# SiLU on ScalarE, six pooled products and alternating score banks in a scan, attention and experts kernel

## The chip, the cores and the metric

The program runs on one core of one Trainium2 chip. The metric is the device time of one launch in microseconds (us), all three stages included. The units of work are TensorE (PE), VectorE (DVE), ScalarE (ACT), GpSimd (POOL) and the DMA queue of SyncE (SP).

## The reference, cut to what matters

The input is 4 images of 64 channels and 1024 positions. Three stages follow each other.

```
for each of 8 sequences (4 images, plain and with the channels shuffled):
    u   = silu(conv(x @ W_in.T) + conv_b)               # 1024 x 128
    B, C, dt_low = u @ W_x.T;  dt = softplus(dt_low @ W_dt.T + b_dt)
    for n in 16 states: h_n[t] = exp(dt*A_n)[t] * h_n[t-1] + (dt*u*B_n)[t]
    y   = (sum over n of h_n * C_n + u * D_skip) * silu(z) @ W_out.T
t = t + causal_attention(layernorm(t))                   # 4 x 1024 x 64
t = t + experts(layernorm(t))                            # attention and feed-forward steps, picked by an argmax
```

## The kernel before

**The scan stage** (`build_scan`) takes the 8 sequences one after the other, and in each the 16 states ("units"). A unit is one 128 x 1024 tile: the channels on the partitions, the positions along the free axis. ScalarE makes the decay exp(dt*A_n) (line 474). The drive dt*u*B_n is made in one of two ways. For the 7 units in `POOLED` GpSimd multiplies a copy of B_n that a DMA has spread over the partitions (line 764); it goes to `dbu`, and the decay then goes to one of the two PSUM tiles `pb`. For the 9 others TensorE spreads B_n into `pb` (line 246), VectorE multiplies it by dtu there (line 618), and the decay goes to one of three `da` tiles. VectorE scans (line 623), GpSimd multiplies by C_n (`hc`, line 753), and TensorE adds the 16 results up in `py` (line 257).

**The next sequence is prepared meanwhile** in two PSUM banks `px`, one for each half of 512 positions, which every step reuses in a fixed order: the convolution (198, 199), Tanh and Identity on ScalarE (409, 410), u on VectorE (582), B and C and their bf16 parts (205 to 218), dt (224 to 230, with 432 to 451 on ScalarE and 589 on VectorE), dt*u (599), then z of the current sequence (236), Tanh (455) and the gate (605). After units 0 to 2 of the next sequence VectorE reads `py` (631). Once in two sequences, at units 13 to 15, TensorE also makes the output of an image (266, 271).

Every engine runs one queue in the order of the code. Each loop over u makes, on its engine, first what the unit needs and then the steps whose `n ==` matches; semaphores hold an engine until its operands are there. TensorE's turn at unit u is: the spread of B for unit u+1 (which waits until scan u-1 is done), the sum of unit u-3, then the steps. ScalarE's is: the decay of u+1, then the steps.

**Attention** (`Attention`, 16 groups of 128 queries, once causal as `l_`, then as `ex_` in the experts). A group's scores for two images fill the two PSUM tiles `s[0]`, `s[1]` (1025 to 1035), VectorE takes the maximum (1100), ScalarE the exponential (1139), TensorE turns the result (1052), VectorE and ScalarE copy it out (1107, 1146), and TensorE multiplies it by the values (1073). In the causal stage group g has g % 8 + 1 blocks of 128 keys.

Of the kernel before, what the change touches and what calls it, by code (L numbers as in the profile page):

```python
# [45 lines left out]
def build_scan(nc, w, inp, scr):  # L46

    ctx = ExitStack()
    with ctx:
# [12 lines left out]
        LAST, UNITS, SKIP_AT = NSEQ - 1, NS * NSEQ, 8  # L62

        u2 = [sb(f"u2_{i}", [DI, L]) for i in range(2)]
        gate = sb("gate", [DI, L])
# [12 lines left out]
        th = sb("th", [DI, L])  # L78
# [11 lines left out]
        x_act, u_done, hi_done, mid_done, lo_done, bcf_done = (  # L90
            sem("x_act"), sem("u_done"), sem("hi_done"), sem("mid_done"), sem("lo_done"), sem("bcf_done"))
        g_act, d_read, e_done, one_done, lost_done, ln_done, dt_done, dtu_done = (
            sem("g_act"), sem("d_read"), sem("e_done"), sem("one_done"), sem("lost_done"),
# [22 lines left out]
        X, BC, BHI, BMID, DT, ADD = range(1, 7)  # L116

        def full(s, piece):
            if s == 0:
                return {X: 1, DT: 2, ADD: 3}[piece]  # L120
            return 7 * s - 4 + outs_before(s - 1) + piece
# [4 lines left out]
        def wait_bc(eng, s, h, piece):  # L126
            if s:
                eng.wait_ge(px_full[h], full(s, piece))
            else:
                eng.wait_ge(bc0_full[h], piece - X)  # L130

        def full_gate(q):
            return full(q + 1, 7) if q < LAST else full(q + 1, 1)

        def full_out(b):
            return full_gate(min(2 * b + 2, LAST)) + 1

        def freed(s, piece):
            return 4 * s - (2 if s else 0) + (outs_before(s - 1) if s else 0) + piece

        def freed_gate(q):
            return freed(q + 1, 3) if q < LAST else freed(q + 1, 0)

        def freed_out(b):
            return freed_gate(min(2 * b + 2, LAST)) + 1

        cst = w["cst"]
        nat = gate[:, :].rearrange("p (s c) -> p s c", c=128)
# [40 lines left out]
        def pe_x(pe, s, h):  # L189
            atleast(pe, px_free[h], freed(s, 0))  # L190
# [30 lines left out]
        def pe_dt(pe, s, h):  # L221
            pe.wait_ge(u_done, 2 * s + h + 1)
            pe.wait_ge(px_free[h], freed(s, 2) if s else 1)
# [9 lines left out]
        def pe_gate(pe, q, h):  # L233
            pe.wait_ge(px_free[h], freed_gate(q))
# [27 lines left out]
        def pe_out_early(pe, b, h):  # L262
            pe.wait_ge(px_free[h], freed_out(b))
            for s in range(2):
# [3 lines left out]
        def pe_out_late(pe, b, h):  # L268
            pe.wait_ge(y_free, 2 * (2 * b + 1) + h + 1)
            for s in range(2):  # L270
# [4 lines left out]
                 (vecs[:, :], 6, w["vcol"][:, 0, :], 1.0), (nat_dt, 128, wdtT, 1.0), (nat[:, NBC, :], 128, w["wbc"][:, :], 0.5)]  # L275
# [1371 lines left out]
```

## Time and profile before

| | us |
|---|---|
| three runs | 811.87, 814.77, 822.22 (median 814.77) |
| the profiled execution, whole | 811.98 |
| its span, first to last instruction | 810.2 |
| TensorE busy | 694.0 (86%) |
| VectorE busy | 592.1 (73%) |
| GpSimd busy | 457.3 (56%) |
| ScalarE busy | 427.7 (53%) |

The scan stage's units run from 47.4 to 491.8 us, causal attention with its norms to about 619 us, the experts to the end. GpSimd has nearly all its work in the first 490 us. The mean granted TensorE clock is 0.975. A busy share over the whole span mixes these stages, so the views below are read stage by stage.

### The profile page before, as it was taken

The page shows a single profiled execution, that of the slowest core. Times are in us where ns is not written, and L with a number is a line of the kernel's source. Part 1 is how long each engine was busy: PE and PEld are TensorE (multiplying, and loading weights), DVE is VectorE, ACT ScalarE, POOL GpSimd, SP SyncE. Part 2 cuts the span into 40 slices and gives each one's busy share as a digit, 9 for nine tenths or more (in the row PEclk, how much of TensorE's full clock was granted, in tenths as well). Part 3 has the DMA queues.
Part 4 walks back from the last instruction along what each step waited for, and adds up shares of the span by engine and source line. Part 5 has one row for each costly group of instructions (what it writes and reads, how often), then busy time and mean ns, then how long its engine had stood idle before and what let it go on. Part 6 is the DMA issues. An engine that isn't in the chain of part 4 may idle for free. (4 is left out here: it accounts for less than half of the span.)

```text
span 810.2 us, 9559 instructions
## 1 busy us (share of the span) xinstructions
PE 694.0 (86%) x3005; PEld 335.9 (41%) x3005; DVE 592.1 (73%) x624; ACT 427.7 (53%) x656; POOL 457.3 (56%) x234
## 2 busy tenths in 40 slices
PE   4769989889999999998898789789983778999993
PEld 2323333333433333333333333367671225677640
DVE  3489999999899998999998981455552334666633
ACT  2868468477485583784763324545443214555520
POOL 6269999999989999899999994000000000000000
PEclk9999999999999999999999999999997799999997
DMA  3398676675566766656766730000000000000001
GB/s 89 85 274 307 223 235 219 210 262 209 193 229 199 253 227 209 208 214 221 253 208 203 251 116 1 0 1 2 2 2 5 8 17 2 2 2 1 2 1 56
DMA packets 32588, 105.33 MB, mean 130 GB/s; under 512 B 6533, under 2 KB 7182, under 8 KB 32526
## 3 DMA queue, kind: packets, MB, share of 16 engines
q1 hardware_dynamic: 31558, 103.91, 38.3%
q10 hardware_dynamic: 648, 0.55, 0.3%
q8 instruction: 28, 0.46, 0.2%
q0 software_dynamic: 320, 0.13, 0.1%
q14 instruction: 34, 0.28, 0.1%
HBM read 98.80 MB, written 2.10 MB: 125 GB/s over the span
## 5 line engine op out<-in xcount | busy, mean ns | idle before, releaser
L753 POOL TENSOR_TENSOR hc<-hh,cc 128x1024 f32<-128x1024 f32 x128 | 298.9, 2351 | 13.3 <-PE py L257 6.6
L257 PE MATMUL py<-hc,w_cst 128*128 128x512 f32 x512 | 239.7, 596 | 5.7 <-DVE yg L631 4.6
L623 DVE TENSOR_TENSOR_SCAN hh<-da,pb 128x1024 f32<-128x1024 f32 x72 | 164.6, 2286 | 2.5
L257 PEld LDWEIGHTS py<-hc,w_cst 128*128 128x128 f32 x512 | 96.0, 190 | 107.9 <-issue 92.2
L623 DVE TENSOR_TENSOR_SCAN hh<-pb,dbu 128x1024 f32<-128x1024 f32 x56 | 127.5, 2277 | 8.7 <-ACT pb L474 5.2
L764 POOL TENSOR_TENSOR dbu<-bb,dtu 128x1024 f32<-128x1024 f32 x56 | 131.6, 2350 | 0.0
L474 ACT ACTIVATE pb<-dt,w_aneg 128x1024 f32<-128x1024 f32 x56 | 62.5, 1116 | 86.3 <-DVE hh L623 84.5
L618 DVE TENSOR_TENSOR pb<-pb,dtu 128x1024 f32<-128x1024 f32 x72 | 87.6, 1217 | 5.5 <-PE pb L246 3.3
L474 ACT ACTIVATE da<-dt,w_aneg 128x1024 f32<-128x1024 f32 x72 | 81.3, 1140 | 0.4
L246 PE MATMUL pb<-bc,w_sel 128*128 128x512 bf16 x144 | 43.5, 384 | 26.6 <-DVE hh L623 24.5
L1423 POOL MEMSET wa<- 128x128 f32 x4 | 0.6, 212 | 111.8 <-POOLq L1176 111.8
L1100 DVE TENSOR_REDUCE ex_nm<-ex_s 128x1 f32<-128x1024 f32 x32 | 37.7, 1219 | 16.4 <-PE ex_s L1025 16.4
L246 PEld LDWEIGHTS pb<-bc,w_sel 128*128 128x128 bf16 x144 | 10.9, 97 | 75.2 <-DVE hh L623 53.3
L1146 ACT ACTIVATE ex_pts<-ex_pt 128x512 f32<-128x512 f32 x32 | 17.4, 595 | 43.2 <-PE ex_pt L1052 43.2
L1139 ACT ACTIVATE ex_p<-ex_s,ex_nm 128x1024 f32<-128x1024 f32 x32 | 35.4, 1120 | 4.8 <-DVE ex_nm L1100 4.8
L1052 PE MATMUL ex_pt<-w_cst,ex_p 128*128 128x128 f32 x256 | 34.9, 280 | 2.8 <-ACT ex_p L1139 1.8
L1107 DVE COPY ex_pts<-ex_pt 128x512 f32<-128x512 f32 x32 | 20.6, 686 | 21.1 <-PE ex_pt L1052 21.1
L1052 PEld LDWEIGHTS ex_pt<-w_cst,ex_p 128*128 128x128 f32 x256 | 27.5, 141 | 17.7 <-issue 14.5
L1025 PE MATMUL ex_s<-ex_kt,ex_qt 64*128 64x512 f32 x128 | 33.5, 644 | 0.9 <-DVE ex_kt L1007 0.9
L1443 PE MATMUL ex_s<-w_h,w 64*128 64x512 f32 x64 | 19.9, 731 | 16.7 <-DMA b<-in_ffn_b 10.4
L479 ACT ACTIVATE w_xm<-px 64x512 f32<-64x512 f32 x8 | 4.7, 591 | 49.5 <-PE px L271 49.5
L1100 DVE TENSOR_REDUCE l_nm<-l_s 128x1 f32<-128x128 f32 (+7 forms) x32 | 22.8, 753 | 9.9 <-PE l_s L1035 9.8
(289 smaller groups left out, 1037.1 us busy)
## 6 DMA issues: line engine op xcount, KB each, us to landing
cc<-scr SPq DMA_DIRECT2D x128, 512.0 KB, 4.2
bb<-scr SPq DMA_DIRECT2D x56, 512.0 KB, 4.9
w_xs<-hc SPq DMA_DIRECT2D x6, 256.0 KB, 4.6
w_xst<-in_x SPq DMA_DIRECT2D x2, 512.0 KB, 5.2
scr<-bcf SPq DMA_DIRECT2D x8, 128.0 KB, 4.3
w_xs<-dt SPq DMA_DIRECT2D x4, 256.0 KB, 6.2
w_xs<-dtu SPq DMA_DIRECT2D x4, 256.0 KB, 6.3
out<-yy SPq DMA_DIRECT2D x4, 256.0 KB, 3.7
```

The costliest lines, as they stand in the source:

```text
L246: last = nc.tensor.matmul(pb[u % 2][:, half(h)], w["sel"][:, n, :], bc3[q % 2][:, half(h)], start=True, stop=True)
L257: nc.tensor.matmul(py[:, half(h)], ident, hc[u % NHC][:, half(h)], start=(n == 0), stop=(n == NS - 1)).then_inc(hc_used, 1)
L474: nc.scalar.activation(to[:, :], dt[q % 2][:, :], ACT.Exp, scale=w["aneg"][:, n:n + 1]).then_inc(da_done, 1)
L618: nc.vector.tensor_tensor(pb[u % 2][:, :], pb[u % 2][:, :], dtu[q % 2][:, :], ALU.mult).then_inc(dbu_done, 1)
L623: nc.vector.tensor_tensor_scan(hh[u % NHH][:, :], decay[:, :], drive[:, :], 0.0, ALU.mult, ALU.add).then_inc(scan_done, 1)
L753: nc.gpsimd.tensor_tensor(hc[u % NHC][:, :], hh[u % NHH][:, :], cc[u % NCC][:, :], ALU.mult).then_inc(hc_done, 1)
L764: nc.gpsimd.tensor_tensor(dbu[k % NDB][:, :], bb[k % 2][:, :], dtu[q % 2][:, :], ALU.mult).then_inc(pooled_done, 1)
L1025: last = nc.tensor.matmul(self.s[r][:, a:a + m], self.qt[rows, g * 128:(g + 1) * 128], self.kt[rows, p * L + a:p * L + a + m], start=True, ...
L1052: last = nc.tensor.transpose(self.pt[:, j:j + 128], self.p[g % 2][r][:, j:j + 128], self.w["cst"][:, IDN:IDN + 128])
L1100: self.nc.vector.tensor_reduce(self.nm[:, i:i + 1], self.s[r][:, 0:128 * self.blocks(g)], AX.X, ALU.max, negate=True).then_inc(self.nm_don ...
L1107: self.nc.vector.tensor_copy(self.pts[g % 2][0][:, a:a + m], self.pt[:, a:a + m]).then_inc(self.pts_dve, 1)
L1139: self.nc.scalar.activation(self.p[g % 2][r][:, 0:n], self.s[r][:, 0:n], ACT.Exp, bias=self.nm[:, i:i + 1], accum_out=self.sm[:, i:i + 1]) ...
```

## The change

ScalarE's Silu makes u and the gate from PSUM in one operation each; VectorE's u and gate operations go. Two `gate` tiles take the place of one, since the gate is now made at units 1 and 2 of its own sequence instead of 12 and 13. `POOLED` has 6 units instead of 7. Steps of the preparation are moved to other units, and ScalarE makes two decays at unit 1 and none at unit 2. The factors 0.5 and 0.25 that belonged to the Tanh form go. In causal attention, groups of at most 4 blocks put their scores by turns in either half of `s` and their turned tiles in either half of `pt`, and the scores, maximum and exponential of the next small group come ahead of the turning of this one.

```diff
-        POOLED = (1, 3, 6, 8, 10, 12, 14)
+        POOLED = (1, 4, 6, 9, 11, 14)
-        gate = sb("gate", [DI, L])
+        gate = [sb(f"gate_{i}", [DI, L]) for i in range(2)]
...
         def pe_bc(pe, s, h):
             pe.wait_ge(u_done, 2 * s + h + 1)
             if s:
-                pe.wait_ge(px_free[h], freed(s, 1))
+                pe.wait_ge(g_done, 2 * (s - 1) + h + 1)
...
         def pe_gate(pe, q, h):
-            pe.wait_ge(px_free[h], freed_gate(q))
+            if q < LAST:
+                pe.wait_ge(u_done, 2 * (q + 1) + h + 1)
+            else:
+                pe.wait_ge(px_free[h], freed(NSEQ))
...
@@ TensorE's loop
-                        if n == 0 + h:
+                        if n == 0:
                             pe_x(pe, q + 1, h)
-                        if n == 2 + h:
+                        if n == 3:
                             pe_bc(pe, q + 1, h)
-                        if n == 3 + h:
+                        if n == 4:
                             pe_bc_less_hi(pe, q + 1, h)
-                        if n == 4 + h:
+                        if n == 6:
                             pe_bc_less_mid(pe, q + 1, h)
-                        if n == 5 + h:
+                        if n == 7:
                             pe_dt(pe, q + 1, h)
-                        if n == 9 + h:
+                        if n == 10 + h:
                             pe_dt_add(pe, q + 1, h)
-                    if n == 11 + h:
+                    if n == 1:
                         pe_gate(pe, q, h)
...
         def act_x(act, s, h):
             act.wait_ge(px_full[h], full(s, X))
-            nc.scalar.activation(th[:, half(h)], px[h][:, :], ACT.Tanh, bias=w["hcb"][:, :], scale=0.5)
-            nc.scalar.activation(px[h][:, :], px[h][:, :], ACT.Identity, bias=w["cb"][:, :]).then_inc(x_act, 1)
+            if s >= 2:
+                act.wait_ge(hc_used, 2 * (NS * (s - 2) + SKIP_AT) + 2)
+                act.wait_ge(dtu_done, 2 * (s - 2) + h + 1)
+            nc.scalar.activation(u2[s % 2][:, half(h)], px[h][:, :], ACT.Silu, bias=w["cb"][:, :]).then_inc(u_done, 1)
...
         def act_gate(act, q, h):
             act.wait_ge(px_full[h], full_gate(q))
-            nc.scalar.activation(th[:, half(h)], px[h][:, :], ACT.Tanh, scale=0.5).then_inc(g_act, 1)
+            atleast(act, y_free, 2 * (q - 2) + h + 1)
+            nc.scalar.activation(gate[q % 2][:, half(h)], px[h][:, :], ACT.Silu).then_inc(g_done, 1)
...
@@ ScalarE's start and loop
-            act.preload_act_table_set("exp_and_others")
-            act.wait_ge(small_done, 1)
-            for h in range(2):
-                act_x(act, 0, h)
             act.wait_ge(a_in, 16)
             nc.scalar.activation(w["aneg"][:, :], a_log, ACT.Exp).then_inc(a_exp, 1)
+            for h in range(2):
+                act_x(act, 0, h)
+            act.preload_act_table_set("exp_and_others")
...
-                act_exp(act, u + 1)
+                if u == 0 or n != AHEAD + 1:
+                    act_exp(act, u + 1)
+                if n == AHEAD:
+                    act_exp(act, u + 2)
...
-                        if n == 1 + h:
+                        if n == 1:
                             act_x(act, q + 1, h)
-                        if n == 3 + h:
+                        if n == 4:
                             act_hi(act, q + 1, h)
-                        if n == 4 + h:
+                        if n == 5:
                             act_mid(act, q + 1, h)
-                        if n == 5 + h:
+                        if n == 6:
                             act_lo(act, q + 1, h)
-                        if n == 6 + h:
+                        if n == 8 + h:
                             act_dt(act, q + 1, h)
                             act_one(act, q + 1, h)
-                        if n == 9:
+                        if n == 10:
                             act_ln(act, q + 1, h)
-                        if n == 10 + h:
+                        if n == 11 + h:
                             act_dt_out(act, q + 1, h)
-                    if n == 12 + h:
+                    if n == 2:
                         act_gate(act, q, h)
...
@@ VectorE's loop (dve_u and dve_gate go)
-                        if n == 1 + h:
-                            dve_u(dve, q + 1, h)
-                        if n == 7 + h:
+                        if n == 9 + h:
                             dve_lost(dve, q + 1, h)
-                        if n == 10 + h:
+                        if n == 11 + h:
                             dve_dtu(dve, q + 1, h)
-                    if n == 12 + h:
-                        dve_gate(dve, q, h)
...
@@ Attention, TensorE (VectorE and ScalarE likewise)
+    def small(self, g):
+        return self.causal and 0 <= g < self.GRP and self.blocks(g) <= HALF // 128
+    def ahead(self, g):
+        return self.small(g) and self.small(g - 1)
...
-                self.pe_scores(pe, k, g)
-                self.pe_turn(pe, k, g - 1, 1)
+                if not self.ahead(g):
+                    self.pe_scores(pe, k, g)
+                if not self.small(g - 1):
+                    self.pe_turn(pe, k, g - 1, 1)
             if g >= 2:
                 self.pe_values(pe, k, g - 2)
+            if self.ahead(g + 1):
+                self.pe_scores(pe, k, g + 1)
             self.pe_turn(pe, k, g, 0)
+            if self.small(g):
+                self.pe_turn(pe, k, g, 1)
```

## Rows read from the trace of the kernel before

**Rows 1.** The windows view: two stretches of 60 us, with and without an image's output.
```profile
core 0: us, PE busy (x) PEld busy (x) DVE busy (x) ACT busy (x) POOL busy (x), PEclk, DMA share, GB/s
166.00:226.00 60.00, 57.68 (x143) 23.57 (x142) 55.33 (x37) 37.23 (x49) 55.94 (x25) 1.00 0.67 226
226.00:286.00 60.00, 53.67 (x133) 21.67 (x132) 58.58 (x40) 39.32 (x50) 59.50 (x26) 1.00 0.66 223
```

**Rows 2.** Timeline of VectorE, units 0 to 3: start, duration, engine, line, operation [idle].
```profile
264.78 1.21 DVE L618 TENSOR_TENSOR pb<-pb,dtu 128x1024 f32<-128x1024 f32 x1
...
268.23 2.26 DVE L623 TENSOR_TENSOR_SCAN hh<-pb,dbu 128x1024 f32<-128x1024 f32 x1
270.40 0.66 DVE L582 SCALAR_TENSOR_TENSOR u<-th,px 128x512 f32<-128x512 f32 x1
271.21 1.23 DVE L618 TENSOR_TENSOR pb<-pb,dtu 128x1024 f32<-128x1024 f32 x1
...
275.56 1.29 DVE L631 TENSOR_TENSOR yg<-py,gate 128x512 f32<-128x512 f32 x2 [0.21 <-DVE u L582]
276.76 2.28 DVE L623 TENSOR_TENSOR_SCAN hh<-pb,dbu 128x1024 f32<-128x1024 f32 x1
```

**Rows 3.** Groups by line: the gate operation on VectorE.
```profile
L605 DVE SCALAR_TENSOR_TENSOR gate<-th,px 128x512 f32<-128x512 f32 x16 | 10.6, 662 | 0.0
```

**Rows 4.** Timeline of VectorE, three idle times around an image's output.
```profile
208.55 1.23 DVE L618 TENSOR_TENSOR pb<-pb,dtu 128x1024 f32<-128x1024 f32 x1 [1.09 <-PE pb L246]
...
213.82 2.29 DVE L623 TENSOR_TENSOR_SCAN hh<-pb,dbu 128x1024 f32<-128x1024 f32 x1 [1.72 <-ACT pb L474]
216.62 0.69 DVE L582 SCALAR_TENSOR_TENSOR u<-th,px 128x512 f32<-128x512 f32 x1 [0.50 <-PE py L257]
```

**Rows 5.** Timeline of GpSimd, two products.
```profile
227.67 2.36 POOL L764 TENSOR_TENSOR dbu<-bb,dtu 128x1024 f32<-128x1024 f32 x1
229.99 4.67 POOL L753 TENSOR_TENSOR hc<-hh,cc 128x1024 f32<-128x1024 f32 x2
```

**Rows 6.** Timeline of TensorE: spread of B, sums, convolution, z, output.
```profile
204.11 1.88 PE L271 MATMUL px<-yg,w_wo 128*128 128x512 f32 x4
...
251.17 1.12 PE L236 MATMUL px<-w_xs,w_wg 64*128 64x512 f32 x2
...
261.56 0.59 PE L246 MATMUL pb<-bc,w_sel 128*128 128x512 bf16 x2 [0.54 <-DVE hh L623]
261.99 3.60 PE L257 MATMUL py<-hc,w_cst 128*128 128x512 f32 x8
265.43 1.02 PE L198 MATMUL px<-w_xs,w_wca 128*128 128x512 f32 x2
```

**Rows 7.** Timeline of ScalarE through the preparation of dt.
```profile
236.99 0.69 ACT L432 ACTIVATE ex<-px,w_vcol 128x512 f32<-128x512 f32 x1
...
239.58 1.14 ACT L474 ACTIVATE da<-dt,w_aneg 128x1024 f32<-128x1024 f32 x1
240.62 1.11 ACT L474 ACTIVATE pb<-dt,w_aneg 128x1024 f32<-128x1024 f32 x1
241.75 1.28 ACT L443 ACT_TABLE_LOAD   x1
243.04 1.07 ACT L443 ACTIVATE px<-px 128x512 f32<-128x512 f32 x2
244.13 1.28 ACT L474 ACT_TABLE_LOAD   x1
...
246.48 0.58 ACT L451 ACTIVATE dt<-px 128x512 f32<-128x512 f32 x1
```

**Rows 8.** Timeline of VectorE, the first half of dt*u.
```profile
247.09 0.69 DVE L599 TENSOR_TENSOR dtu<-px,u 128x512 f32<-128x512 f32 x1 [0.29 <-ACT dt L451]
```

**Rows 9.** Timeline of TensorE in causal attention, groups 1 and 3.
```profile
532.86 0.44 PE L1052 MATMUL l_pt<-w_cst,l_p 128*128 128x128 f32 x2 [0.82 <-ACT l_p L1139]
...
540.23 0.66 PE L1052 MATMUL l_pt<-w_cst,l_p 128*128 128x128 f32 x4 [0.44 <-ACT l_p L1139]
```

**Rows 10.** Timelines at the start: u on VectorE, then ScalarE's first step of dt.
```profile
28.24 0.68 DVE L582 SCALAR_TENSOR_TENSOR u<-th,px 128x512 f32<-128x512 f32 x1
```
```profile
30.26 0.69 ACT L432 ACTIVATE ex<-px,w_vcol 128x512 f32<-128x512 f32 x1 [1.43 <-PE px L224]
```

**Rows 11.** Timeline of TensorE, the last sum inside the loop.
```profile
480.07 1.99 PE L257 MATMUL py<-hc,w_cst 128*128 128x512 f32 x4 [0.54 <-POOL hc L753]
```

More of the change, by code:

```diff
@@ L113, in outs_before @@
             return max(0, (q - 1) // 2)
-        X, BC, BHI, BMID, DT, ADD = range(1, 7)
+        X, GATE, BC, BHI, BMID, DT, ADD = range(1, 8)
         def full(s, piece):
@@ L601, in dve_dtu @@
             dve.sem_inc(px_free[h], 1)
-        def dve_gate(dve, q, h):
-            dve.wait_ge(g_act, 2 * q + h + 1)
-            nc.vector.scalar_tensor_tensor(gate[:, half(h)], th[:, half(h)], 1.0, px[h][:, :],
-                                           ALU.add, ALU.mult).then_inc(px_free[h], 1)
         def dve_unit(dve, u):
@@ L949, in blocks, with turn_start, start @@
         return g % 8 + 1 if self.causal else L // 128
+    def small(self, g):
+        return self.causal and 0 <= g < self.GRP and self.blocks(g) <= HALF // 128
+    def turn_start(self, g, r):
+        return HALF * r if self.small(g) else 0
+    def ahead(self, g):
+        return self.small(g) and self.small(g - 1)
+    def start(self, g):
+        return HALF if self.small(g) and g % 2 else 0
     def halves(self, g):
@@ L1018, in pe_scores @@
         pe.wait_ge(self.k_out, 4 * k + 2 * p + (n - 1) // HALF + 1)
-        atleast(pe, self.p_done, 2 * (self.GRP * k + g))
-        plain = n - 128 if self.causal else n
+        atleast(pe, self.p_done, 2 * (self.GRP * k + (g - 1 if self.small(g) and self.small(g - 1) else g)))
+        plain, o = n - 128 if self.causal else n, self.start(g)
         for a in range(0, plain, HALF):
@@ L1024, in pe_scores @@
                 rows = slice(C * r, C * r + C)
-                last = nc.tensor.matmul(self.s[r][:, a:a + m], self.qt[rows, g * 128:(g + 1) * 128],
+                last = nc.tensor.matmul(self.s[r][:, o + a:o + a + m], self.qt[rows, g * 128:(g + 1) * 128],
                                         self.kt[rows, p * L + a:p * L + a + m], start=True, stop=True)
@@ L1045, in pe_turn @@
         for h, (a, m) in enumerate(self.halves(g)):
-            if r == 0:
-                before = self.halves_before(g - 1) + len(self.halves(g - 1)) if g else 0
-                atleast(pe, self.pts_act, 2 * self.GRP * k + before)
-            else:
+            if r == 0 and not (self.small(g) and self.small(g - 1)):
+                atleast(pe, self.pts_act, self.evacs_done(k, g))
+            if r == 0 and self.small(g - 1):
+                atleast(pe, self.pts_dve, self.evacs_done(k, g))
+            if r == 1 and self.small(g):
+                atleast(pe, self.pts_act, self.evacs_done(k, g))
+            if r == 1 and not self.small(g):
                 pe.wait_ge(self.pts_dve, self.evacs_done(k, g) + len(self.halves(g)))
+            o = self.turn_start(g, r)
             for j in range(a, a + m, 128):
-                last = nc.tensor.transpose(self.pt[:, j:j + 128], self.p[g % 2][r][:, j:j + 128],
+                last = nc.tensor.transpose(self.pt[:, o + j:o + j + 128], self.p[g % 2][r][:, j:j + 128],
                                            self.w["cst"][:, IDN:IDN + 128])
@@ L1120, in dve_all @@
                 finish(dve, k, g - 3)
-            for r in range(2):
-                self.dve_max(dve, k, g, r)
+            if not self.ahead(g):
+                for r in range(2):
+                    self.dve_max(dve, k, g, r)
             if g == 0:
@@ L1126, in dve_all @@
                 self.dve_project_v(dve, k, (2,))
+            if self.ahead(g + 1):
+                for r in range(2):
+                    self.dve_max(dve, k, g + 1, r)
             self.dve_turned(dve, k, g)
@@ L1157, in act_all @@
                 self.act_project(act, k, (0, 1))
-            else:
+            elif not self.small(g - 1):
                 self.act_turned(act, k, g - 1)
-            for r in range(2):
-                self.act_exp(act, k, g, r)
+            if not self.ahead(g):
+                for r in range(2):
+                    self.act_exp(act, k, g, r)
             if g == 0:
@@ L1167, in act_all @@
                 self.act_inverse(act, k, g - 2)
+            if self.ahead(g + 1):
+                for r in range(2):
+                    self.act_exp(act, k, g + 1, r)
+            if self.small(g):
+                self.act_turned(act, k, g)
         self.act_turned(act, k, self.GRP - 1)
```

76 lines of the change are left out of this document (34 added, 42 removed).

## The prediction, made before the changed kernel was run

> **What bounds the kernel now.** I read the windows first, then the timeline of each engine over one sequence. In the scan stage three engines are nearly full at once. Without an image's output VectorE is busy 58.6 and GpSimd 59.5 of 60 us; with one, TensorE is at 57.7 and the other two fall to 55 or 56 [rows 1]. So a sequence without output is VectorE's and GpSimd's, one with output TensorE's. VectorE's timeline gives the terms; I take starts to starts, since records overlap by about 0.08. A unit with its own product takes 268.23 - 264.78 = 3.45, a pooled one 270.40 - 268.23 = 2.17, one u half 0.81, both halves of y 1.20 [rows 2]. With 9 and 7 units, two u (1.7), two "lost" and two dt*u at like durations (3.3 with a wait of 0.29, [rows 8]), two gates (1.17, [rows 3]) and y, that is 53.7 us. GpSimd has 23 products at (229.99 - 227.67) = 2.32, 53.3 us [rows 5]. Around an output VectorE waits 1.09 + 1.72 + 0.50 = 3.3 us more [rows 4].
>
> **What is removed and added on VectorE.** u goes from the loop for 7 sequences: 14 halves at 0.81 to 0.88, 11.8 us. The gate goes: 16 x (0.66 - 0.08) = 9.3 us. Eight units become own units: 8 x (3.45 - 2.17) = 10.2 us come in. Net -10.9 us. GpSimd loses 8 products, 18.6 us, and falls to 22 x 2.32 = 51.0 a sequence; VectorE's bare work is 51.8. TensorE gets one more spread of B, 0.43 [rows 6], a sequence. So the whole change hangs on waits: can the other engines deliver at VectorE's new places? I walk one sequence, time 0 being the multiplication of unit 0.
>
> **The wait before y (new).** TensorE starts x of the next sequence 0.65 after that zero now (265.43 against 264.78, [rows 2, 6]) and would again. Both halves now stand at n = 0, 4 x 0.86 = 3.44, until 4.1. Then come the spread for unit 2 (0.43), the sum of unit 14 (eight matmuls take 3.44 for two units, so 1.72), two z matmul pairs at 1.06 (8.4), the spread for unit 3 (8.8) and the sum of unit 15 (10.5, its result 0.16 later). Silu isn't late for it: decays 1 to 3 end at 3.3, a function-set load 1.28 makes 4.6 and two halves of about 0.6 end at 5.9, while z asks at 6.2 [rows 6, 7]. VectorE is ready for y at 3.45 + 2.17 + 3.45 = 9.1; the second half of y can start at 10.7, so unit 3 starts at 11.35 where 10.3 was possible. Cost 1.06 in each of the 4 boundaries without output: 4.2 us. It was about nothing before, since z stood at units 11 and 12 and x's second half behind the spread. Unit 4's decay is ready at 11.5, wanted at 14.8: the two extra set loads hide there.
>
> **The wait before dt*u (larger).** Now the second "lost" has units 9 and 10 behind it before dt*u, 5.6 us for Ln, a set load, a decay and the copy of dt. After the change it has only unit 11, pooled, 2.17. ScalarE's chain starts with the decay of pooled unit 9, which waits for the end of scan 7 (0.12 past the start of unit 8). From there: 1.05, four dt operations 2.6 (239.58 - 236.99), 1.04, 2.6, 1.05, load 1.3, two Ln 1.08, load 1.3, decay 1.05, copy 0.6 = 13.7 [rows 7]; ready at 13.8. VectorE is there after 3.45 + 2.17 + 0.58 + 3.45 + 0.58 + 2.17 = 12.4. It waits 1.4 in place of 0.3 to 0.36, +1.06 in each of 7 sequences: 7.4 us. Other operations of unknown place in this chain I bound by 0 (Ln's first load could overlap a wait) and 1.3 (one load more in line).
>
> **Outputs.** From the spread of unit 15 TensorE has, in its order: 0.43 + 1.72 + 1.72 (output, [rows 6]) + 1.9 (skip, taken as the same row) + 0.43 + 1.72 + 1.72 + 1.72 + 3.44 (x) = 14.8 before the spread for unit 2, against 11.3 of VectorE's units 14, 15, 0, 1. The stalls become about 0.9 (unit 0), 1.7 (the decay of unit 1, behind ScalarE's copy of the output), 1.7 (unit 2) and 2.1 at y. That is 6.3 against 3.3 and the small wait in u, +2.9 for the two boundaries with x behind them: +5.7. At the last one there is no x; -0.3. The moved z doesn't help: the spread for 15 waits for scan 13 anyway.
>
> **The tail.** In the last sequence GpSimd sets the end. From unit 3's end it has 14 products, 32.4 us, to hc of unit 12, 1.1 earlier against that unit than now [rows 5, 11]; early output, three sums and y follow unchanged. -1.1 us.
>
> **The start.** Silu takes two operations out of the path to u, and dt starts when ScalarE has reloaded: squares end at 24.5, load 25.8, halves at 26.5 and 28.2, load 29.5, where 30.26 stands now; u itself was at 28.24 [rows 10]. -0.8 us (0 to -1.5).
>
> **Attention.** TensorE's idle before turning goes where scores are made ahead: 0.82, 0.45 and 0.44 in groups 1 to 3, some 1.0 in 9 to 11 [rows 9]. At groups 4 and 12 the second turning no longer covers the maximum and exponential, about 0.5 each. -1.7 us (0 to -3).
>
> **Sum.** -10.9 + 4.2 + 7.4 + 5.7 - 0.3 - 1.1 - 0.8 - 1.7 = +2.5. On the profiled execution's 811.98 that is 814.5, say 814. It lies at the lower edge of the runs shown; their median is 2.8 above it, and I leave the forecast at 814. A measurement of this kernel tells 2% (16 us) from no change.
>
> **Rival 1: the waits are absorbed.** If TensorE and ScalarE keep the lead they have now (y and dt*u wait 0.2 to 0.3), the 4.2, 7.4 and 5.7 go and 798 remains; with half, 806. For it: ScalarE is only 38 us busy in 60 [rows 1]. Against it: it is late by order, not by load. **Rival 2: slower.** A switch of function sets costs more than its record: ScalarE would lie idle behind it. There are four switches a sequence instead of two; the two in the dt chain fall wholly on VectorE's wait once that exists, the Silu one on z and y. If each cost 2.6 instead of 1.3, the dt wait grows by 2.6 and that of y by about 0.4, 3 us x 7 = 21 us: 835. It decides from about 2.3 us a switch on. Against it: the decay ends at 240.62 + 1.11 = 241.73, the load starts at 241.75, Ln at 243.04 [rows 7]; nothing is lost beside 1.28. **Rival 3: it doesn't do what it says**: Silu slower than Tanh's 0.69, or one set serving Exp and Ln. The latter takes a load out of the dt wait, 7 x 1.28 = 9 us: 805. Against it: today's trace loads again after every Ln [rows 7].
>
> The Trainium skill speaks against this change: "ScalarE: Activation LUTs", What ACT_TABLE_LOAD costs, gives 1283 ns for the load and some 1380 ns of drain, 2.66 us for each switch. By that rule rival 2 holds and the time would be about 835. Here the load agrees, while no drain is seen between the records.
>
> **Chances.** Forecast (808 to 820): 0.55. Rival 1, in part or whole: 0.3, of which 0.08 is beyond -2%. Rival 2 or a stall of that size: 0.07. Rival 3: 0.08, within 2%. The range reaches to rival 1 on one side and on the other to the upper bound of the dt chain (7 x 1.3 = 9 over the forecast): 798 to 824. Faster by over 2% 0.09, within 0.85, slower 0.06.
>
> **What would show it.** On VectorE: wait before y near 1 us (2 after an output), wait before dt*u near 1.4 by ScalarE's dt, unit 2 after an output held by the spread of B. Four set loads a sequence. u and gate gone, 80 multiplications of line 618's kind. If y and dt*u wait under 0.4, rival 1 is right; idle behind the loads shows rival 2. My walk is wrong if TensorE gets ahead of it, for instance because an order of steps was misread, or if GpSimd's spare time is used up (pooled drives are ready only 0.6 to 0.9 before they are wanted).

## The result and the profile after

The changed kernel takes 825.6 us (median of 4 runs, 824.81 to 830.29), the kernel before 814.16 us (4 runs, 811.87 to 822.22). The ratio is 1.013, 95% interval 1.008 to 1.018: slower by 1.3%, where 814 was forecast and 824 was the upper bound. The profiled execution took 825.3 us, its span is 823.5.

The page's busy times say nothing alarming: VectorE has less to do (592.1 before), GpSimd less (457.3), and TensorE 6.9 us more.

```profile
PE 700.9 (85%) x3021; PEld 342.3 (42%) x3021; DVE 582.9 (71%) x599; ACT 440.7 (54%) x657; POOL 439.9 (53%) x226
```

The windows of the same two stretches as [rows 1] show two things. VectorE fell from 55.3 and 58.6 to 51.4 and 55.5 us of 60, GpSimd with it, so both now wait. And PEclk, the granted TensorE clock, is 0.97 where it was 1.00.

```profile
166.00:226.00 60.00, 56.26 (x136) 23.11 (x136) 51.38 (x32) 37.15 (x46) 50.59 (x23) 0.97 0.58 194
226.00:286.00 60.00, 53.55 (x129) 21.94 (x128) 55.54 (x36) 40.04 (x50) 54.49 (x24) 0.97 0.59 202
```

Four stretches, each cut at rows found in both timelines, sum to the difference of the spans:

| stretch | before | after | |
|---|---|---|---|
| start, to VectorE's first multiplication of unit 0 | 47.37 | 46.69 | -0.7 |
| recurrence, to the first y operation of the last sequence | 442.84 | 456.99 | +14.2 |
| causal attention with its norms, to the first router product | 129.40 | 126.26 | -3.1 |
| experts, to the first of the last four VectorE operations | 182.24 | 179.66 | -2.6 |
| end of the program | 8.35 | 13.90 | +5.6 |

The forecast of the recurrence was +5.0 (-10.9 + 4.2 + 7.4 + 5.7 - 0.3 - 1.1). So 9.2 us are missing there, and 5.6 at the end. The -2.6 of the experts isn't the change's: with the same code in that stage the profiles below show 179.1 to 184.8 us. The waits of VectorE from 40 to 500 us (engine, what was waited for, total, times, longest) name the places:

```profile
DVE dtu L598 <- ACT dt L456: 10.8, 10, 1.5
DVE pb L612 <- PE pb L248: 9.4, 8, 1.6
DVE yg L625 <- PE py L259: 9.0, 12, 1.5
DVE hh L617 <- ACT pb L480: 5.2, 3, 1.7
```

Before, these were 2.0, 3.3, nearly nothing before the last y, and 5.2. The timeline of VectorE around an output, and in a sequence without one, answers to [rows 4, 2, 8]:

```profile
211.62 1.23 DVE L612 TENSOR_TENSOR pb<-pb,dtu 128x1024 f32<-128x1024 f32 x1 [1.63 <-PE pb L248]
...
216.90 2.29 DVE L617 TENSOR_TENSOR_SCAN hh<-pb,dbu 128x1024 f32<-128x1024 f32 x1 [1.72 <-ACT pb L480]
220.57 1.23 DVE L612 TENSOR_TENSOR pb<-pb,dtu 128x1024 f32<-128x1024 f32 x1 [1.38 <-PE pb L248]
...
225.60 0.69 DVE L625 TENSOR_TENSOR yg<-py,gate 128x512 f32<-128x512 f32 x1 [1.48 <-PE py L259]
...
255.71 0.69 DVE L598 TENSOR_TENSOR dtu<-px,u 128x512 f32<-128x512 f32 x1 [1.40 <-ACT dt L456]
...
276.23 1.23 DVE L612 TENSOR_TENSOR pb<-pb,dtu 128x1024 f32<-128x1024 f32 x1 [0.58 <-PE pb L248]
281.25 0.69 DVE L625 TENSOR_TENSOR yg<-py,gate 128x512 f32<-128x512 f32 x1 [1.48 <-PE py L259]
```

The stall for dt is 1.40, as walked. Around the output they are 1.63 + 1.72 + 1.38 + 1.48 = 6.2 in sum, where 6.3 was walked. But y waits 1.48 also without an output (in three of the four such places; at 165 us it is 0.59), and the 0.58 before unit 2 is new. Those two are TensorE's, and TensorE's own timeline shows why:

```profile
252.28 1.13 PE L228 MATMUL px<-ex,w_cst 128*128 128x512 f32 x2 [2.89 <-ACT px L448]
...
264.44 0.84 PE L248 MATMUL pb<-bc,w_sel 128*128 128x512 bf16 x2 [2.44 <-DVE hh L617]
265.07 3.38 PE L259 MATMUL py<-hc,w_cst 128*128 128x512 f32 x4
268.29 0.60 PE L248 MATMUL pb<-bc,w_sel 128*128 128x512 bf16 x2
```

It idles 2.89 us for ScalarE's logarithm (0.28 before) and soon 2.44 us for VectorE, which itself had waited for dt. Behind that, four float matmuls take 3.38 us, where they take 1.88 elsewhere. The granted clock in that piece, 264.4 to 268.2, is 0.55 by the windows view (1.00 from 268.3 on), near the lower of the clock's two levels, 1.2 GHz of 2.4. From there to 281 TensorE has no idle time, at a granted clock of 1.00, so the x and z products that stand ahead of y are still late from that piece. A piece of this kind stands in each of the seven sequences that prepare another, those with an output too (0.62 from 192 to 196 us). ScalarE's own timeline is the walked chain:

```profile
241.89 1.12 ACT L480 ACTIVATE pb<-dt,w_aneg 128x1024 f32<-128x1024 f32 x1 [0.46 <-DVE hh L617]
...
249.24 1.10 ACT L480 ACTIVATE pb<-dt,w_aneg 128x1024 f32<-128x1024 f32 x1
250.35 1.28 ACT L448 ACT_TABLE_LOAD   x1
251.65 1.07 ACT L448 ACTIVATE px<-px 128x512 f32<-128x512 f32 x2
252.74 1.28 ACT L480 ACT_TABLE_LOAD   x1
254.04 1.15 ACT L480 ACTIVATE da<-dt,w_aneg 128x1024 f32<-128x1024 f32 x1
255.09 0.58 ACT L456 ACTIVATE dt<-px 128x512 f32<-128x512 f32 x1
```

### The profile page after: what moved, and what is told of

Its sections match the earlier page's. It is cut to its first block and busy times, and to the rows that moved or that the text cites. A ratio compares the mean times of both kernels' runs of the same rounds, so it can differ in the third digit from the quotient of the medians.

```text
span 823.5 us, 9541 instructions
## 1 busy us (share of the span) xinstructions
PE 700.9 (85%) x3021; PEld 342.3 (42%) x3021; DVE 582.9 (71%) x599; ACT 440.7 (54%) x657; POOL 439.9 (53%) x226
## 5 line engine op out<-in xcount | busy, mean ns | idle before, releaser
L259 PE MATMUL py<-hc,w_cst 128*128 128x512 f32 x512 | 245.9, 611 | 0.9 <-POOL hc L740 0.4
L617 DVE TENSOR_TENSOR_SCAN hh<-da,pb 128x1024 f32<-128x1024 f32 x80 | 182.9, 2287 | 2.8
L259 PEld LDWEIGHTS py<-hc,w_cst 128*128 128x128 f32 x512 | 100.4, 198 | 103.4 <-issue 83.4
L617 DVE TENSOR_TENSOR_SCAN hh<-pb,dbu 128x1024 f32<-128x1024 f32 x48 | 109.0, 2271 | 6.3 <-ACT pb L480 5.2
L751 POOL TENSOR_TENSOR dbu<-bb,dtu 128x1024 f32<-128x1024 f32 x48 | 113.0, 2355 | 0.0
L612 DVE TENSOR_TENSOR pb<-pb,dtu 128x1024 f32<-128x1024 f32 x80 | 97.4, 1217 | 12.0 <-PE pb L248 9.4
L480 ACT ACTIVATE da<-dt,w_aneg 128x1024 f32<-128x1024 f32 x80 | 89.5, 1140 | 1.2
L480 ACT ACTIVATE pb<-dt,w_aneg 128x1024 f32<-128x1024 f32 x48 | 53.6, 1116 | 67.5 <-DVE hh L617 66.5
L248 PE MATMUL pb<-bc,w_sel 128*128 128x512 bf16 x160 | 51.0, 402 | 28.2 <-DVE hh L617 26.0
L1113 DVE TENSOR_REDUCE ex_nm<-ex_s 128x1 f32<-128x1024 f32 x32 | 37.7, 1220 | 14.7 <-PE ex_s L1028 14.7
L1467 PE MATMUL ex_s<-w_h,w 64*128 64x512 f32 x64 | 19.7, 718 | 17.7 <-DMA b<-in_ffn_b 11.5
L228 PE MATMUL px<-ex,w_cst 128*128 128x512 f32 x32 | 17.5, 631 | 19.5 <-ACT px L448 19.5
```

Of the source, the lines that this page charges most:

```text
L248: last = nc.tensor.matmul(pb[u % 2][:, half(h)], w["sel"][:, n, :], bc3[q % 2][:, half(h)], start=True, stop=True)
L259: nc.tensor.matmul(py[:, half(h)], ident, hc[u % NHC][:, half(h)], start=(n == 0), stop=(n == NS - 1)).then_inc(hc_used, 1)
L480: nc.scalar.activation(to[:, :], dt[q % 2][:, :], ACT.Exp, scale=w["aneg"][:, n:n + 1]).then_inc(da_done, 1)
L612: nc.vector.tensor_tensor(pb[u % 2][:, :], pb[u % 2][:, :], dtu[q % 2][:, :], ALU.mult).then_inc(dbu_done, 1)
L617: nc.vector.tensor_tensor_scan(hh[u % NHH][:, :], decay[:, :], drive[:, :], 0.0, ALU.mult, ALU.add).then_inc(scan_done, 1)
L751: nc.gpsimd.tensor_tensor(dbu[k % NDB][:, :], bb[k % 2][:, :], dtu[q % 2][:, :], ALU.mult).then_inc(pooled_done, 1)
```

## The experiments

Theory: two faults of one origin. The serial chain on ScalarE (exponential, set load, logarithm, set load, decay, dt) is exposed, and the idle time that it leaves on TensorE costs granted clock, which makes y and the spread late. Rivals: it is the order on TensorE alone (x and z ahead of y), or GpSimd's missing products, or the new attention. "Loop" below is the second stretch of the table, 442.84 before and 456.99 after; "y to y" is the time between the first y operations of two sequences, 53.8 without and 57.4 with an output before, 55.7 (once 54.6) and 60.5 after. The tail is the last such interval, 48.4 before and 48.8 after. They come from one profiled execution each; two executions of unchanged recurrence code differ in them by 1.1 (before and e6) and 2.5 us (after and e7), so a smaller difference carries nothing by itself. Ratios are to the kernel before, run on the same chip.

**e1: one table set for Exp and Ln.**
```diff
                     if n == 2:
                         act_gate(act, q, h)
+                        if h == 1:
+                            act.preload_act_table_set("natural_log_exp_and_others")
```


> The changed kernel, but ScalarE loads the set that has both Exp and Ln right after the gate, so that the two function-set loads around Ln in each sequence go (4 loads a sequence become 2). Theory A (the wait before dt*u is ScalarE's serial chain, and TensorE's clock falls because this chain leaves it idle twice): the chain is 2.6 us shorter, VectorE's wait before dt*u falls from 1.4 to about 0.1, TensorE's idle before line 228 from 2.9 to about 1.6, the clock stays at its upper level, and the wait at y falls from 1.48 to 1.06: some 7 x 2.5 = 17 us less, ratio to the kernel before 0.990 to 0.996. Rival B (the clock has nothing to do with this chain): only 7 x 1.3 = 9 us less, 1.002, granted clock unchanged at 0.96. Rival C (a switch is hidden, ScalarE isn't on the path): no change, 1.013.

Measured: 813.89 us, ratio 0.997 (0.993 to 1.000), some 12 us below the changed kernel. In the waits of VectorE the line of dt is gone, and TensorE's wait for the logarithm falls from 19.5 (longest 2.9) to 9.6 us (longest 1.5). Loop 442.1, down 14.9: the 10.8 of dt's wait, and 4 us more that VectorE used to wait for TensorE. Of these, 1.4 lie in the tail (last section), and the stall of unit 0 behind an output is 1.03 where it was 1.63. But the clock isn't held, as theory A had it: without an output y still waits 1.47 in three of four places, behind sums of four matmuls that take 3.0 to 3.4 us, and the granted clock of the loop is 0.98. The groups of ScalarE's loads from 40 to 500 us, after and then e1, show half of them gone:

```profile
L480 ACT ACT_TABLE_LOAD x15 | 19.2, 1283 | 0.3
L415 ACT ACT_TABLE_LOAD x7 | 9.0, 1283 | 0.1
L448 ACT ACT_TABLE_LOAD x7 | 9.0, 1283 | 0.1
```
```profile
L581 ACT ACT_TABLE_LOAD x8 | 10.3, 1283 | 0.1
L415 ACT ACT_TABLE_LOAD x7 | 9.0, 1283 | 0.1
```

**e2: dt*u one unit later.**
```diff
-                        if n == 11 + h:
+                        if n == 12 + h:
                             dve_dtu(dve, q + 1, h)
```


> The changed kernel, but VectorE multiplies dt*u one unit later (n = 12 + h), so that units 11 and 12 cover ScalarE's chain. Theory A: the wait of 1.4 goes (7 x 1.4 = 10 us). TensorE's idle before line 228 stays at 2.9, its second idle before the spread for unit 13 becomes shorter by 1.4; if both are needed for the clock to fall, the clock stays and another 5 to 8 us go: ratio 0.992 to 0.996; if the first is enough, 1.001. Rival B (clock unrelated): 1.001 with the clock at 0.96. Rival C (the wait only moves elsewhere, to the next sequence's first unit): 1.010 or more.

Measured: 817.54 us, ratio 1.001 (0.998 to 1.005), loop 449.1. VectorE no longer waits for dt, but it waits 16.6 us for the spread (12 times, longest 2.6) where it waited 9.4. TensorE's wait for the logarithm stays, at 19.0, and the granted clock of the loop stays at 0.97. Some 8 us are back (1.4 of them in the tail), for the price of the new waits: moving the reader out of the way of a late chain doesn't mend the chain.

**e3: TensorE kept busy.** Eight matmuls of zeros behind the sums of units 10 and 12 in each sequence but the last; the chain on ScalarE is untouched.
```diff
+        def pe_fill(q, count):
+            for i in range(count):
+                h = i % 2
+                nc.tensor.matmul(py[0:96, half(h)], w["less"][:, 1, 0:96], bc3[q % 2][:, half(h)], start=False, stop=False,
...
+                if n == 10 and q < LAST:
+                    pe_fill(q, 8)
+                if n == 12 and q < LAST:
+                    pe_fill(q, 8)
```


> The changed kernel with 16 more matmuls a sequence that add zeros to the running sum in PSUM, 8 before dt is added (n = 10) and 8 after the sum at n = 12, about 1.7 us each, in TensorE's idle times; nothing else is moved. Theory A (the idle times cost TensorE its clock, and the slow stretch delays the next sequence's first units): granted clock of the scan stage back to 1.00, the 0.6 us wait at unit 2 goes, y's wait falls from 1.48 to 1.06, no 0.5 us wait of the multiplication behind dt*u; the wait before dt*u stays at 1.4: 7 x 1.0 to 1.4 = 7 to 10 us less, ratio 1.001 to 1.005. Rival B (the clock falls by load or at random): clock at 0.96 still, 1.013. Rival C (more matmuls only delay the queue): 1.015 or more.

Measured: 821.7 us, ratio 1.005 (1.000 to 1.009); loop 450.7, down 6.3; granted clock of the loop 0.99. TensorE does more and the kernel isn't slower; by the ratios it is faster than the changed kernel (1.013), but the two intervals touch, and what shows the gain is the rows. In the place of the rows at 264 us above, its timeline now has the normal durations:

```profile
263.05 0.38 PE L248 MATMUL pb<-bc,w_sel 128*128 128x512 bf16 x1 [0.94 <-DVE hh L627]
263.26 1.88 PE L259 MATMUL py<-hc,w_cst 128*128 128x512 f32 x4
265.09 0.59 PE L248 MATMUL pb<-bc,w_sel 128*128 128x512 bf16 x2
```

The wait for dt is what it was, 1.39. Without an output y waits 0.59 instead of 1.48, and the 0.58 of unit 2 is gone:

```profile
254.09 0.69 DVE L608 TENSOR_TENSOR dtu<-px,u 128x512 f32<-128x512 f32 x1 [1.39 <-ACT dt L466]
...
278.05 0.69 DVE L635 TENSOR_TENSOR yg<-py,gate 128x512 f32<-128x512 f32 x1 [0.59 <-PE py L259]
```

y to y is 54.07 without an output, and 60.53, unchanged, with one. Of the 6.3 us, 4.9 lie in the first sequence (1.2) and in those without an output. The 4.9 are against one execution of the changed kernel: against e7, whose scan code is the same as the changed kernel's, they are 2.4, because there y waits 1.47 in one place of four without an output and 0.59 in the others. With an output two things cancel: the second half of dt*u no longer waits (up to 0.39 before), and unit 0 waits 1.80 to 2.15 instead of 1.63, behind the zeros. The other 1.4 lie in the tail, where no zeros stand, and aren't this edit's (see the last section).

**e4: x and z spread over two units again.**
```diff
-                        if n == 0:
+                        if n == 0 + h:
                             pe_x(pe, q + 1, h)
...
-                    if n == 1:
+                    if n == 1 + h:
                         pe_gate(pe, q, h)
```


> The changed kernel, but TensorE makes the second half of the convolution at unit 1 and the second half of z at unit 2, behind the sum that y waits for, instead of both halves at once. Theory A (y and unit 2 wait because TensorE's order puts 1.7 us of convolution ahead of the spread for unit 2 and 1.1 us of z ahead of the last sum): the wait at unit 2 goes (0.58, after an output 1.38), the wait at y falls by 1.1: 4 x 1.5 + 3 x 2.4 = 13 us less, ratio 0.995 to 1.000; the clock stays at 0.96. Rival B (ScalarE's Silu and its set load are late then, since z's second half comes later): the decay of unit 4 is late and unit 4 waits about 1 us: 1.003 to 1.008. Rival C (y waits for GpSimd's product, not for TensorE's order): 1.013.

Measured: 826.76 us, ratio 1.013 (1.007 to 1.019). The expected gain of 13 us isn't there. The loop is 4.2 us shorter in its profile (452.8, which belongs to a run of 816.56, the fastest of five), so the median leaves no gain to speak of; 1.4 of the 4.2 are the tail's. The ratio is the one that rival C gave, but not by its cause: wherever y waits, the releaser is TensorE's sum. The stall of unit 2 behind an output went, and y's wait there grew from 1.48 to 2.71: all of x and the first half of z still stand ahead of the last sum, and a wait that has two readers only changed hands. dt's wait stayed, at 11.5.

**e5: e1 and e3 together.**

> The changed kernel with both remedies that worked alone: ScalarE's table set that serves both the exponential and the logarithm is loaded once for the softplus of a sequence (two loads a sequence instead of four), and TensorE gets eight matmuls of zeros at units 10 and 12 so that it is never long idle. Theory A (the loss has two independent parts, the serial softplus chain on ScalarE, and TensorE's granted clock that falls after idle times): both add up, the last sequence's first output product comes at about 486 us of the span (488.0 with the table set alone), granted clock of the recurrence 1.00 (0.98), the wait of VectorE before y falls from 1.5 to about 0.6 in the sequences without an output; time about 812. Theory B (with the chain shortened TensorE is no longer idle long enough to matter, and the remaining waits are of order, not of clock): the matmuls of zeros only stand in the way, first output product at 488 or later, time 814 or more.

Measured: 804.56 us, ratio 0.985 (0.979 to 0.990), 21 us below the changed kernel. Loop 441.5, y to y 52.66 in all three sequences without an output and 59.1 with one. Against e3 this is e1's edit alone once more: the loop is 9.3 us shorter for 14 loads fewer, 10.7 up to the tail, which is 1.4 us longer here than in e3. Where both loads stood (250.35 and 252.74 above) ScalarE now goes from decay to logarithm directly; its idle time there is for VectorE:

```profile
241.82 1.10 ACT L490 ACTIVATE pb<-dt,w_aneg 128x1024 f32<-128x1024 f32 x1
242.86 0.54 ACT L458 ACTIVATE px<-px 128x512 f32<-128x512 f32 x1
244.74 0.58 ACT L458 ACTIVATE px<-px 128x512 f32<-128x512 f32 x1 [1.33 <-DVE ex L600]
```

Around an output, with TensorE at its normal durations throughout, three of the four stalls are what they were in the changed kernel: 1.72, 1.38 and 1.48. Those are TensorE's and ScalarE's order. The first isn't: it is 1.79 to 2.15 here, behind the zeros, and 1.03 in e9, which has no zeros there. VectorE's rows of unit 0 in e5, then in e9:

```profile
204.21 1.23 DVE L624 TENSOR_TENSOR pb<-pb,dtu 128x1024 f32<-128x1024 f32 x1 [2.15 <-PE pb L248]
```
```profile
203.82 1.23 DVE L624 TENSOR_TENSOR pb<-pb,dtu 128x1024 f32<-128x1024 f32 x1 [1.03 <-PE pb L248]
```

**e6: the attention part alone**, on the kernel before (the diff's hunks of the class of attention, from `small` to `act_turned`, and no other).

> The kernel before with only the attention part of the change (small causal groups alternate between two halves of the score banks); the recurrence is that of before. Theory A (it takes away the waits of TensorE between small groups and nothing else): the causal attention, from the last sequence's first y to the first router product, takes 126.3 us as in the changed kernel and not 129.4; the recurrence keeps its intervals of 53.7 and 57.4 us; the time is 3 us below before, 811 to 812. Theory B (the new order in attention also causes the later end of the program, 13.9 us instead of 8.4 from the last VectorE product to the end of the span): the end takes about 14 us, and the time is 2 to 3 us above before, 817.

**e7: the recurrence part alone** (all the other hunks).

> The changed kernel with the attention of before: only the recurrence part of the change. Theory A (the loss is in the recurrence alone, +13.5 us up to the last sequence's y, and the end of the program is drawn at either of two levels in any kernel): y of the last sequence at 503.7, causal attention 129.4, end 8 or 14 us, time 826 to 829. Theory B (the later end comes with the new attention): end about 8.3 us, time 823.

Measured: e6 811.33 us, ratio 0.995 (0.991 to 0.998); e7 827.83 us, ratio 1.014 (1.008 to 1.021). Attention is 126.15 us in e6 and 130.5 in e7, against 126.26 after and 129.40 before. Over all profiles with the new order it is 126.1 to 126.3 where the granted clock of this stretch is 1.00, and 127.5 to 127.9 where it is 0.98; with the old order 129.4 at 1.00 and 130.5 at 0.98 (e7). At like clock that is a gain of its own of some 3 us. The end of the program is 8.05 us in e6 and 13.59 in e7, so the later end doesn't come with the new attention. The product of the two ratios, 1.009, and the changed kernel's 1.013 agree within their intervals.

**e8: e1 with 7 products on GpSimd.**
```diff
-        POOLED = (1, 4, 6, 9, 11, 14)
+        POOLED = (1, 4, 6, 8, 10, 12, 14)
```


> The changed kernel with the table set that serves exponential and logarithm, and with GpSimd making 7 of the 16 products again (units 1, 4, 6, 8, 10, 12, 14), so VectorE sheds eight products of 1.22 us. Theory A (VectorE's work bounds the recurrence once the waits are small, as 1.0 us a product): 8 x 1.2 = 9.8 us less than the run with the table set alone (813.9), 804 to 806, y of the last sequence at 478 to 480. Theory B (with fewer products on VectorE the waits that its work now covers return: TensorE's spread, ScalarE's chain, and GpSimd's product comes late for the scan): 3 us less or nothing, 811 to 814, with new waits of the scan on GpSimd's product.

Measured: 811.37 us, ratio 0.992 (0.988 to 0.996), 2.5 us below e1 by the medians, not 10; and the loop is 446.8, 4.7 longer than e1's, half of it in the tail, which GpSimd bounds. VectorE's work fell by eight products and its waits took their place; the one for GpSimd's product was 1.1 in e1:

```profile
DVE hh L619 <- POOL dbu L753: 15.0, 27, 1.9
```

**e9 and e10: where and how many zeros.** e9 is e5 with the zeros only in the sequences without an output; e10 is e5 with four and four instead of eight and eight.
```diff
-                if n == 10 and q < LAST:
+                if n == 10 and q < LAST and (q % 2 or q == 0):
```


> The version with the single table set and the matmuls of zeros (804.6 us), with the matmuls of zeros only in the four sequences without an output. Theory A (TensorE is full enough by itself where it makes an output; there the zeros only stand ahead of it): sequences without an output keep 52.7 us, those with one come back from 59.1 and 56.1 to 58.0 and 55.0, the last sequence's y 3.3 us earlier, at 484.2; time 801 to 802. Theory B (the zeros also hold the clock in sequences with an output): intervals there 59 us or more, granted clock of the recurrence back to 0.98, no gain or a loss, 804 to 808.

> The version with the single table set, with four matmuls of zeros at units 10 and 12 instead of eight. Theory A (what matters is that no long idle time of TensorE is left; four fill 0.9 of it): clock of the recurrence 0.99, intervals 52.7 and 58.6, time 803 to 805. Theory B (four don't cover it): some of TensorE's matmuls run at twice their time again, intervals of 54 us in sequences without an output as in the run without the zeros, time 809 or more.

Measured: e9 800.51 us, ratio 0.981 (0.975 to 0.986), y to y 52.66 and 58.0 to 58.4, loop 438.0, granted clock 1.00. e10 806.53 us, ratio 0.987 (0.981 to 0.993), loop 441.8. With an output the zeros only stood in the way: those intervals are 0.8 to 1.1 shorter without them, and 1.4 of the 3.5 us between the loops of e5 and e9 is the tail's. Four zeros keep the 52.66 between the later sequences as eight do, but in the first sequence four matmuls take 3.46 us again and y waits 1.47.

**e11: e9 with z behind the last sum.**
```diff
-                    if n == 1:
+                    if n == 2:
                         pe_gate(pe, q, h)
```


> The run before last (single table set, zeros only in sequences without an output), with TensorE's gate products (1.98 us a sequence) at unit 2, behind the last sum of the sequence before, and no longer at unit 1 ahead of it. Theory A (VectorE's wait before y is TensorE's work that stands ahead of the last sum: the next sequence's u product of 4.1 us and the gate product of 2.0 us): the wait before y falls from 0.5 to nothing without an output and from 1.6 to nothing with one, 0.5 x 4 + 1.6 x 3 = 6.8 us less if nothing else is late: 795 to 797. Theory B (the wait moves: the gate's SiLU comes a unit later, and the B/C products that wait for it, then the chain behind them): TensorE waits before the B/C products, the spread of unit 3 or 4 comes late for VectorE, and the time stays within 2 us of the run without the move.

Measured: 800.28 us, ratio 0.978 (0.972 to 0.985), the lowest median of all, though not told apart from e9. The loop is 433.6, 4.4 us shorter than e9's, though its tail is 1.4 longer. All waits before y are gone but the last sequence's own, also behind an output:

```profile
DVE yg L637 <- PE py L259: 8.3, 2, 8.2
```

In this profile attention took 127.7 and the experts 182.5 us, against 126.1 and 179.6 in e9's, with the same code in both. That is where the 4.4 us went between these two profiles. The granted clock of the attention is 0.98 in this one and 1.00 in e9's, that of the experts 0.93 and 0.94; what lowers it there is open.

## Why the prediction was wrong

**VectorE's work** (-10.9) was right: 51.8 us of bare work a sequence were forecast, and e3's 54.07 less its waits (1.39, 0.59 and the later second half of y) is 51.8. **The wait before dt*u** was right in kind and a little small: it waited 1.40 as walked, but 10.8 us in all, with up to 0.39 at some second halves, where there were 2.0 before. That is +8.8 for +7.4.

**The wait before y** (1.06, +4.2) is the step that failed. The walk took TensorE's durations as fixed at their rows of before, all read at full clock. Its order was read correctly: from the multiplication of unit 0 to that of unit 3 it had 11.35 us, and with the clock held, in e3, it is 279.51 - 268.31 = 11.20. In the changed kernel it is 282.72 - 269.93 = 12.79. The walk asked only whether TensorE would be *late*, never what it does while it *waits*. The same ScalarE chain whose 1.4 us the prediction charged to VectorE leaves TensorE idle for 2.9 us (0.28 before) and again for 2.4, and behind them its matmuls take close to twice their time. That adds 0.89 before y and 0.58 before unit 2 wherever the piece stands close ahead of them: in three of four places in this execution, in one of four in e7's. In all it is 4.9 of the 9.2 us missing in the loop by e3, and 2.4 if e3 is held against e7. **The tail**, forecast at -1.1, gave +0.4 (48.79 from y to y against 48.38): its sums fell into a piece of low clock too, and the last y waits 8.16 us instead of 6.73. Where they did not, as in e3, the tail is 47.37 us, the -1.0 that was forecast. So this 1.4 us is the same failed step, told below.

**Outputs** hold the other 2.9. By the prediction's terms an interval with an output and x behind it should take 57.42 - 1.57 + 1.06 + 2.9 = 59.8 us, and the last one 56.0; they took 60.5, 60.5 and 57.5. The sum of the four stalls, 6.2 against 6.3, came out by luck: unit 0 waits 1.63 where 0.9 was walked (at the last output too, where -0.3 was forecast), unit 2 1.38 for 1.7 and y 1.48 for 2.1; the second half of dt*u, which was in no term, waits up to another 0.39. Ahead of unit 0 stands a piece of low clock, and with neither this piece nor the long chain, in e1 and e9, unit 0 waits 1.03. How the 0.6 between them splits, no run shows.

**The start** was forecast at -0.8 and gave -0.7 (u now made by 28.46, dt's first step at 29.77 where 30.26 stood [rows 10]). **Attention** gave -3.1 for -1.7, just outside its range of 0 to -3; e6 and e7 show it apart. The idle rows of 0.82 and 0.44 [rows 9] are gone in the small groups; the first turnings now stand behind scores:

```profile
544.47 0.71 PE L1038 MATMUL l_s<-w_cst 128*128 128x128 f32 x4
545.02 0.38 PE L1059 MATMUL l_pt<-w_cst,l_p 128*128 128x128 f32 x2
```

**The end of the program**, +5.6 us, was in no term. Without it the profiled execution would have been at 819.7, inside the range; without the 9.2 of the loop, too. Against them stand attention (1.4 better than forecast) and the experts (2.6, in no term), and that gives the 10.8 us by which this execution lies above 814.5.

**Rival 1** (waits absorbed) isn't what happened, but nearly its time can be had by other edits: e9 and e11 are at 800. **Rival 3** looked for one set that serves both functions in the changed kernel as it stands; it isn't used there, but one line asks for it. Its price, 9 us of dt wait, is about right (e5 against e3: 9.3 us of the loop, 10.7 without the tail). e1 gained 14.9: dt's 10.8, the tail's 1.4, and the rest mostly at the outputs. **Rival 2** was a right sign with a wrong cause. In the chain above the load starts 0.01 after the decay ends and the logarithm 0.02 after the load, 1.28 for each switch and nothing beside it. The Trainium skill ("ScalarE: Activation LUTs", What ACT_TABLE_LOAD costs) speaks of 2.66 us for a switch with its drain. By that figure I estimate up to 37 us for the 14 loads that e5 has fewer than e3. They were worth 9.3, but that alone decides nothing, since the wait in which they stood was 1.4 us a sequence. What decides is the rows: no drain of some 1.4 us is seen between these records, so the trace doesn't bear this part of the page out here, and the loss didn't need it.

## What to carry to other kernels

When a change lengthens a serial chain on one engine, list every engine that idles for it, not only the one that is late, and for TensorE ask what the granted clock will be behind the idle time; durations read at full clock are a lower bound. Take a second profile of the same code before dividing up a few microseconds: the loops of two profiles of the same scan code differed by 2.5 us (after and e7), with the slow pieces in other places. A handful of harmless matmuls placed only where such an idle time stands was worth more than it cost (e5 against e9 for where, e3 for how much), and a table set that serves two alternating functions is the first thing to look for. Moving a reader (e2) or splitting a block of work (e4) handed the wait to the next reader; taking the work out of the chain (e1) or putting it behind the operation that was waited for (e11) removed it.

## What the runs showed of the hardware

**The clock falls behind some idle times of 2 to 3 us and not behind others.** In the changed kernel the piece at half speed stood behind idle times of 2.89 and 2.44 us with 9.7 us of work between them. In the tail a wait of 2.6 us, with waits of 1.59 and 0.59 us ahead of it, falls out either way. TensorE's timeline in e9, then in e5, whose last sequences have the same instructions:

```profile
471.34 0.60 PE L248 MATMUL pb<-bc,w_sel 128*128 128x512 bf16 x2 [2.63 <-DVE hh L629]
471.78 3.85 PE L259 MATMUL py<-hc,w_cst 128*128 128x512 f32 x8
```
```profile
473.62 0.60 PE L248 MATMUL pb<-bc,w_sel 128*128 128x512 bf16 x2 [2.63 <-DVE hh L629]
474.06 5.29 PE L259 MATMUL py<-hc,w_cst 128*128 128x512 f32 x8
```

e1, e2, e3, e4 and e9 had the quick form (6.73 us before the last y, a tail of 47.4), the changed kernel, e5, e7, e10 and e11 the slow one (8.2 and 48.8). The quick ones aren't free of slow pieces: each has eight matmuls of a sum that take 5.29 us instead of 3.6 earlier in its tail, in e9 at 441.66, where they cost the last y nothing; e5 and e10 have them in both places. Nor did the change bring this in. The profile of the kernel before shows no such piece from 52 us to the end of the loop, with idle times of up to 2.46 us, but e6, which has the same scan code, shows two, behind 2.46 and 2.16 us. The rows of before, then of e6, at the same place in the tail:

```profile
441.97 0.61 PE L246 MATMUL pb<-bc,w_sel 128*128 128x512 bf16 x2 [2.16 <-DVE hh L623]
442.64 1.96 PE L257 MATMUL py<-hc,w_cst 128*128 128x512 f32 x4
```
```profile
442.89 0.60 PE L246 MATMUL pb<-bc,w_sel 128*128 128x512 bf16 x2 [2.16 <-DVE hh L623]
443.56 3.65 PE L257 MATMUL py<-hc,w_cst 128*128 128x512 f32 x4
```

The granted clock from 443.5 to 447.1 us is 1.00 in before and 0.53 in e6, whose tail is 1.1 us longer. What decides between the two forms I can't say. A wait of that length is a risk, of 1.4 us at the last y, not a price.

**The end of the program has two lengths.** From the first of the last four VectorE operations to the end of the span it is 7.9 to 8.5 us in before, e4, e5, e6, e8, e9, e10 and e11, and 12.9 to 14.7 in after, e1, e2, e3 and e7. In the changed kernel the engine that comes last there is TensorE: the last instruction of its queue (DRAIN, in front of the barrier that closes the program) stands 5.4 us behind SyncE's, though its last matmul is some 16 us back. In e5 it stands ahead of SyncE's. The source view of that line, after and then e5 (shortest, median and longest ns, then the start in us):

```profile
L1328 SPq DRAIN  x1: 7/7/7, 817.9 to 817.9; - x1
L1328 PEldq DRAIN  x1: 13/13/13, 823.3 to 823.3; - x1
```
```profile
L1340 PEldq DRAIN  x1: 13/13/13, 801.5 to 801.5; - x1
L1340 SPq DRAIN  x1: 7/7/7, 802.4 to 802.4; - x1
```

In e1, e2, e3 and e7 TensorE's stands 3.6 to 4.9 us behind SyncE's too, and SyncE's wait for TensorE's queue at this line is 3.8 to 5.6 us in all five long ones and at most 0.5 in the others. The long ones also have more transfers of the instruction queue in the last 17 us, 5 packets against 2 or 3. The DMA view of the last 17 us (packets, MB, share), after and then e5:

```profile
q8 instruction: 5, 0.08, 1.8%
```
```profile
q8 instruction: 2, 0.03, 0.8%
```

The new attention isn't its cause (e5 has it and ends early, e7 lacks it and ends late), nor is a slow recurrence (e4 is slow and ends early, e1 is quick and ends late). Within one kernel the times also fall into two clusters some 7 us apart: e3 has three runs at 812.2 to 816.8 and seven at 820.4 to 823.5. That would fit an end that is drawn in each execution, but only the profiled ones show their end, and no experiment addressed it. Why TensorE's queue is late there stays open, and so does how much of the 1.3% is owed to it: the profiles say 5.6 of 13.3 us.
